# Attention with keys split ahead, score passes of 256 columns, and values one step later on TensorE

## What is computed

```python
q = layernorm(x); k = v = ctx_2048            # (16, 128, 256)
scores = einsum('bhqd,bhkd->bhqk', q, k) * 16 ** -0.5
scores = where(key > query, -inf, scores)
out = einsum('bhqk,bhkd->bhqd', softmax(scores), v)
x = x + tanh(g_xattn[1]) * out
```

## Time and profile before

| | us |
|---|---|
| median of 3 runs | 922.41 (921.37 to 923.53) |
| profiled execution | 921.7 |
| its span in the trace | 919.9 |

### The profile page before, as it was taken

One profiled execution on the slowest core, in us unless ns is written; L12 is line 12 of the kernel. 1 busy time (PEld: TensorE's weight loads), 2 busy tenths in 40 slices (PEclk: granted clock), 3 DMA queues, 4 the chain that ended last, 5 costly groups with the idle time before them and its releaser, 6 DMA issues.

```text
span 919.9 us, 13780 instructions
## 1 busy us (share of the span) xinstructions
PE 888.2 (97%) x4704; PEld 711.0 (77%) x4704; DVE 604.5 (66%) x1238; ACT 550.3 (60%) x955; POOL 191.7 (21%) x163
## 2 busy tenths in 40 slices
PE   6799999999999999989999989999999999999997
PEld 5699887787888888756666667878788888888886
DVE  6699764465645656598898776657765465665554
ACT  3225353434543344468888766777777877777774
POOL 5799200000000102067776420000000000000000
PEclk8899999999999999999999999999999999999999
DMA  8203150442211532135553334434444344444443
GB/s 299 76 14 121 41 149 18 132 121 81 74 53 50 182 104 64 40 115 172 173 165 126 113 96 140 124 121 141 133 150 143 102 134 144 145 138 147 150 127 103
DMA packets 62564, 108.54 MB, mean 118 GB/s; under 512 B 7808, under 2 KB 18432, under 8 KB 62112
## 3 DMA queue, kind: packets, MB, share of 16 engines
q1 hardware_dynamic: 61776, 107.53, 37.0%
q10 hardware_dynamic: 720, 0.14, 0.1%
HBM read 103.13 MB, written 4.52 MB: 117 GB/s over the span
## 4 chain that ended last, share of the span: by engine, by line
PE 84%; DVE 6%; ACT 3%; POOL 2%; DMA 2%; issue 2%; SPq 0%; DVEq 0%; ACTq 0%; POOLq 0%
PE bank L666 37%; PE bank L702 29%; PE bank L1470 2%; PE bank L1481 2%; PE bank L1153 1%; PE bank L1152 1%; PE bank L1150 1%; PE bank L1166 1%; PE bank L365 1%; PE bank L1463 1%; DMA k_blocks_sb<-in_k_blk 1%; PE bank L1462 1%; PE bank L1458 1%; DMA x_mixed<-in_x 1%; PE bank L346 1%
## 5 line engine op out<-in xcount | busy, mean ns | idle before, releaser
L465 ACT ACTIVATE y_hi<-y 128x512 fp32r<-128x512 f32 x200 | 124.1, 621 | 81.3 <-DVE y L546 80.7
L560 DVE TENSOR_TENSOR y<-y,gate_rows 128x512 f32<-128x512 f32 x124 | 85.8, 692 | 120.4 <-ACT y L454 118.2
L702 PE MATMUL bank<-y_hi,w_hi 128*128 128x512 f32 x400 | 157.3, 393 | 1.5 <-DVE y_lo L311 1.0
L702 PE MATMUL bank<-y_lo,w_hi 128*128 128x512 f32 x400 | 156.7, 392 | 0.0
L702 PE MATMUL bank<-y_hi,w_lo 128*128 128x512 f32 x400 | 156.1, 390 | 0.0
L311 DVE TENSOR_TENSOR y_lo<-y,y_hi 128x512 fp32r<-128x512 f32 x196 | 134.4, 686 | 29.9 <-ACT y_hi L465 29.6
L448 ACT ACTIVATE activated<-bank 128x512 f32<-128x512 f32 x136 | 81.1, 597 | 80.8 <-PE bank L666 76.2
L666 PE MATMUL bank<-x_hi_first,w_hi 128*128 128x512 f32 x264 | 106.3, 403 | 0.7 <-DVE w_lo L306 0.7
L666 PE MATMUL bank<-x_hi_first,w_lo 128*128 128x512 f32 x264 | 104.3, 395 | 0.0
L666 PE MATMUL bank<-x_lo_first,w_hi 128*128 128x512 f32 x264 | 104.2, 395 | 0.0
L666 PE MATMUL bank<-x_hi_last,w_hi 128*128 128x512 f32 x264 | 104.0, 394 | 0.0
(11 more groups left out here) (155 smaller groups left out, 1436.5 us busy)
## 6 DMA issues: line engine op xcount, KB each, us to landing
gate_rows<-gates SPq DMA_DIRECT2D x156, 256.0 KB, 3.7
w_raw<-in_wu SPq DMA_DIRECT2D x68, 256.0 KB, 2.6
k_blocks_sb<-in_k_blk SPq DMA_DIRECT2D x64, 256.0 KB, 4.6
w_raw<-in_wu SPq DMA_DIRECT2D x32, 384.0 KB, 3.2
v_slot<-in_v_rows SPq DMA_DIRECT2D x16, 256.0 KB, 2.6
ctx_windows<-in_ctx_win SPq DMA_DIRECT2D x3, 1024.0 KB, 10.8
toeplitz<-in_kpad SPq DMA_DIRECT2D x4, 512.0 KB, 9.1
x_mixed<-in_x SPq DMA_DIRECT2D x4, 512.0 KB, 9.2
```

Source lines behind the costliest of these rows:

```text
L465: act.activation(mem.yhi[:, K % S, :], mem.y[:, K % S, :], ACT.Copy).then_inc(s_yh, 1)
L560: dve.tensor_tensor(mem.y[:, K % S, :], mem.y[:, K % S, :], gate, ALU.mult).then_inc(s_yd, 1)
L702: last = pe.matmul(acc(s)[:, c, :], w_[:, Nu % S, wc], y_[:, K % S, :], start=(n == 0 and m == 0), stop=(n == U - 1 and m == 2), skip_grou ...
```

## The change

The keys are no longer split in the attention. The host passes them compactly (`k_rows`, 128 x 256 a block). In units 16 to 42 of `f0` they are loaded two blocks at a time into the slots of the values, rounded by ScalarE (`split_hi`), differenced by GpSimd (`split_lo`) and both parts are stored to DRAM (`k_parts`), four transfers each time. GpSimd sets the eight key slots to zero once. For a quad, `load_keys` now brings two 64-partition pieces of 64 KB, each part's rows repeated twice (by a step of zero in the source), into the non-zero halves; the slot is used by TensorE as it lands, and is free again after its scores.

The split of the work over the 128 rows changes with it: rows hold two heads, each with both parts of the keys against both parts of the query (which is laid out twice). So a score pass covers two heads, 256 columns, with its own stationary queries, and a quad has two of them in place of two of 512. The queries have two sets a = 0, 1, so there are two groups of four transposes and two copies per batch in place of one; they are now float32r transposes with a rounded identity. Rounding and difference of the queries are over 512 elements, before 256.

TensorE's order in step n becomes turns of n, scores of n+2, values of n-1. Of the query's groups, set 0 of b+2 stands at t = 3, set 1 of b+1 at t = 0. On ScalarE the query copies stand ahead of the exponential at t = 0 and 1, and the output copy behind it.

```diff
-                    if not final and K == NK - 16:
-                        attention_loads(sp)
+                    if not final:
+                        if K in (16, 18):
+                            load_raw(sp, (K - 16) // 2)
+                        if 21 <= K < 45 and K % 3 == 0:
+                            i = (K - 21) // 3
+                            store_parts(sp, i)
+                            if i + 2 < NB // 2:
+                                load_raw(sp, i + 2)
+                        if K == NK - 16:
+                            attention_loads(sp)
+                        if NK - 16 <= K < NK - 16 + KR:
+                            load_keys(sp, K - NK + 16)
...
+                    for i in range(NB // 2):
+                        split_lo(pool, i)
+                    blocks_zeroed(pool)
...
+                        if 19 <= K < 43 and K % 3 == 1:
+                            split_hi(act, (K - 19) // 3)
...
-        KLR, KR, SR, DR, PR = 6, 4, 3, 3, 3
+        KR, SR, DR, PR = 8, 3, 3, 3
...
-        KM = sb("k_blocks_sb", [P, KLR, 4 * P])
-        K1 = sb("k_blocks_hi", [P, KR, 4 * P], F32R)
-        K2 = sb("k_blocks_lo", [P, KR, 4 * P], F32R)
+        K1 = sb("k_blocks", [P, KR, 4 * P], F32R)
+        ident_r = sb("ident_r", [P, P], F32R)
+        xc = sb("xn_c", [P, 2, D])
         V = sb("v_slot", [P, 2, NH1, 32])
-        xc = sb("xn_c", [P, 2, D])
-        xs = sb("xn_split", [P, 2, 4, 2, 64], F32R)
-        Q1 = sb("q_split_t", [P, 2, 4, P], F32R)
+        xs = sb("xn_split", [P, 2, 4, 2, P], F32R)
+        Q1 = sb("q_split_t", [P, 2, 2, 4, P], F32R)
...
+        def split_places(i):
+            parts = xs[:, i % 2].rearrange("p t a f -> p (t a f)")
+            return V[:, i % 2].rearrange("p h d -> p (h d)"), parts[:, 0:2 * D], parts[:, 2 * D:4 * D]
+        def load_raw(sp, i):
+            if i >= 2:
+                sp.wait_ge(s_k2, i - 1)
+            sp.dma_start(split_places(i)[0].rearrange("p (b f) -> p b f", b=2),
+                         k_rows[2 * i:2 * i + 2].rearrange("b p f -> p b f")).then_inc(s_kr[i % 2], 16)
+        def split_hi(act, i):
+            act.wait_ge(s_kr[i % 2], 16 * (i // 2 + 1))
+            if i >= 2:
+                act.wait_ge(s_ks[i % 2], 64 * (i // 2))
+            raw, high, _ = split_places(i)
+            act.activation(high, raw, ACT.Copy).then_inc(s_k1, 1)
+        def split_lo(pool, i):
+            pool.wait_ge(s_k1, i + 1)
+            raw, high, low = split_places(i)
+            pool.tensor_tensor(low, raw, high.bitcast(F32), ALU.subtract).then_inc(s_k2, 1)
+        def store_parts(sp, i):
+            sp.wait_ge(s_k1, i + 1)
+            sp.wait_ge(s_k2, i + 1)
+            for part, rows in enumerate(split_places(i)[1:]):
+                for j in range(2):
+                    place = k_parts[2 * i + j].rearrange("(g s d) f -> g s d f", s=2, d=HD1)[:, part]
+                    sp.dma_start(place, rows[:, j * D:(j + 1) * D].bitcast(F32)).then_inc(s_ks[i % 2], 16)
+        def blocks_zeroed(pool):
+            pool.memset(K1[:].rearrange("p n f -> p (n f)").bitcast(F32), 0.0).then_inc(s_kz, 1)
         def load_keys(sp, n):
-            if n >= KLR:
-                sp.wait_ge(s_k2, n - KLR + 1)
-            sp.dma_start(KM[:, n % KLR, :], k_blk[n]).then_inc(s_kl[n % KLR], 16)
+            if n >= KR:
+                sp.wait_ge(s_s, n - KR + 1)
+            for hh in range(2):
+                first = k_parts.offset + (2 * P * (n // 4) + 64 * (n % 4) + 32 * hh) * D
+                place = bass.AP(k_parts.tensor, first, [[D, 2 * HD1], [0, 2], [1, D]])
+                sp.dma_start(K1[64 * hh:64 * hh + 64, n % KR, hh * D:hh * D + D].bitcast(F32), place).then_inc(s_kl[n % KR], 16)
 
         def load_values(sp, b):
             if b >= 2:
                 sp.wait_ge(s_pv, 4 * (b - 2) + 4)
             sp.dma_start(V[:, b % 2].rearrange("p h d -> p (h d)"), v_rows[b]).then_inc(s_vl[b % 2], 16)
-        def key_hi(act, n):
-            act.wait_ge(s_kl[n % KLR], LOADED + 16 * (n // KLR + 1))
-            if n >= KR:
-                act.wait_ge(s_s, n - KR + 1)
-            act.activation(K1[:, n % KR, :], KM[:, n % KLR, :], ACT.Copy).then_inc(s_k1, 1)
-        def key_lo(pool, n):
-            pool.wait_ge(s_k1, n + 1)
-            pool.tensor_tensor(K2[:, n % KR, :], KM[:, n % KLR, :], K1[:, n % KR, :].bitcast(F32),
-                               ALU.subtract).then_inc(s_k2, 1)
 
         def query_normed(act, b):
             act.wait_ge(s_sh, b // (2 * BPB) + 1)
@@ -1354,36 +1398,46 @@
             act.activation(xc[:, b % 2, :], X[:, b, :], ACT.Identity, bias=nshift[:, b:b + 1],
                            scale=rstd[:, b:b + 1]).then_inc(s_n, 1)
 
+        def copies_of(view):
+            return view.rearrange("p (g f) -> p g f", f=HD1).unsqueeze(2).broadcast_to((P, NH1, 2, HD1))
+        def part_rows(b, part):
+            return xs[:, b % 2].rearrange("p t a (h d f s) -> p (t a h) d f s", h=2, d=2, s=2)[:, :, :, :, part]
         def query_hi(act, b):
             act.wait_ge(s_n, b + 1)
             if b >= 2:
-                act.wait_ge(s_xt, b - 1)
-            act.activation(xs[:, b % 2, :, 0, :], xc[:, b % 2, :].rearrange("p (q f) -> p q f", q=4),
-                           ACT.Copy).then_inc(s_hi, 1)
+                act.wait_ge(s_xt, 2 * (b - 1))
+            else:
+                act.wait_ge(s_ks[b], 64 * (NB // 4))
+            act.activation(part_rows(b, 0), copies_of(xc[:, b % 2, :]), ACT.Copy).then_inc(s_hi, 1)
 
         def query_lo(pool, b):
             pool.wait_ge(s_hi, b + 1)
-            pool.tensor_tensor(xs[:, b % 2, :, 1, :], xc[:, b % 2, :].rearrange("p (q f) -> p q f", q=4),
-                               xs[:, b % 2, :, 0, :].bitcast(F32), ALU.subtract).then_inc(s_lo, 1)
-        def query_turned(pe, b):
+        def query_turned(pe, b, a):
...
-                last = pe.transpose(x_bank[:, t * P:(t + 1) * P],
-                                    xs[:, b % 2, t].rearrange("p s f -> p (s f)").bitcast(F32), ident[:])
+                last = pe.transpose(x_bank[:, t * P:(t + 1) * P].bitcast(F32R), xs[:, b % 2, t, a, :], ident_r[:])
...
+            act.wait_ge(s_xt, 2 * b + a + 1)
             if b >= 2:
                 act.wait_ge(s_s, 4 * (b - 1))
-            act.activation(Q1[:, b % 2].rearrange("p t q -> p (t q)"), x_bank, ACT.Copy, scale=SCALE1).then_inc(s_qt, 1)
+            act.activation(Q1[:, b % 2, a].rearrange("p t q -> p (t q)"), x_bank, ACT.Copy, scale=SCALE1).then_inc(s_qt, 1)
...
-            for n in range(KLR):
-                load_keys(sp, n)
+            for i in range(2):
+                sp.wait_ge(s_ks[i], 64 * (NB // 4))
+            sp.wait_ge(s_kz, 1)
...
-            if left in (12, 11, 4):
-                query_normed(act, {12: 0, 11: 1, 4: 2}[left])
-            if left in (11, 10, 3):
-                query_hi(act, {11: 0, 10: 1, 3: 2}[left])
-            if left in (9, 8, 7, 6):
-                key_hi(act, 9 - left)
-            if left in (6, 3):
-                query_copy(act, {6: 0, 3: 1}[left])
+            if left == 16:
+                act.activation(ident_r[:], ident[:], ACT.Copy).then_inc(s_ir, 1)
+            if left in (15, 13, 4):
+                query_normed(act, {15: 0, 13: 1, 4: 2}[left])
+            if left in (14, 12, 3):
+                query_hi(act, {14: 0, 12: 1, 3: 2}[left])
+            if left in (10, 7, 4, 1):
+                query_copy(act, (10 - left) // 6, (10 - left) // 3 % 2)
...
-            if left in (8, 5):
-                query_turned(pe, {8: 0, 5: 1}[left])
+            if left in (12, 9, 6, 3):
+                query_turned(pe, (12 - left) // 6, (12 - left) // 3 % 2)
...
-                pe.wait_ge(s_k2, n + 1)
+                pe.wait_ge(s_kl[n % KR], LOADED + 32 * (n // KR + 1))
                 if t == 0:
-                    pe.wait_ge(s_qt, b + 1)
-                pe.matmul(s_bank(n), Q1[:, b % 2, t, :], K1[:, n % KR, :], start=False, stop=False)
-                pe.matmul(s_bank(n), Q1[:, b % 2, t, :], K2[:, n % KR, :], start=False, stop=True).then_inc(s_s, 1)
+                    pe.wait_ge(s_qt, 2 * b + 2)
+                blocks = K1[:, n % KR, :].rearrange("p (h a k) -> p h a k", h=2, a=2)
+                for a in range(2):
+                    last = pe.matmul(s_bank(n)[:, a * 2 * P:(a + 1) * 2 * P], Q1[:, b % 2, a, t, :], blocks[:, :, a, :],
+                                     start=False, stop=(a == 1))
+                last.then_inc(s_s, 1)
...
-                    if n + KR < NQ:
-                        key_lo(pool, n + KR)
...
                     turned(pe, n)
                     if n + 2 < NQ:
                         scores(pe, n + 2)
-                    if n == 0:
+                    if n == 1:
                         pe.wait_ge(f0.s_xa, 5)
-                    if n < NQ - 1:
-                        values(pe, n)
+                    if n > 0:
+                        values(pe, n - 1)
...
```

(43 more changed lines are left out.)

17 lines of the change are left out of this document (10 added, 7 removed).

## The result

| | kernel before | changed kernel |
|---|---|---|
| median | 922.48 us (921.37 to 923.53) | 906.98 us (906.16 to 910.07) |
| ratio to before, 95% interval | | 0.9842 [0.9823, 0.9862] |
| profiled execution, its span | 921.7, 919.9 | 910.07, 908.3 |

The gain is 15.5 us where 11.4 were forecast; 907.0 lies inside the range and outside the forecast's own 908 to 914. So the two traces lie 11.6 us apart where the medians lie 15.5 apart.

What follows compares the result with a forecast made beforehand. The attention step was held bound by the 1.70 us latency chain turns, exponential, values, with TensorE close behind. Passes and order 17.4, query groups -6.2, key splitting 1.0, feed-forward -0.9 gave 11.3 us: forecast 911.0, range 904 to 920.

Steps and rivals of the forecast that it cites:

- The chain of 1.70: Attention step bound by turns, exponential, values, turns: 0.70 + 0.60 + 0.05 + 0.35 = 1.70 us; step becomes 1.40.
- The price of a query group: Attention: a group of four rounded query transposes taken at 0.44 us; 14 more groups cost 6.2 us.
- rounded transposes fast: Rival, chance 0.12: query transposes cost 0.06 us each, 5.7 us less over 27 groups, about 906.
- The sum: Whole kernel: 17.4 - 6.2 + 1.0 - 0.9 = 11.3 us gained; profiled 921.7 to 910.4, median 911.0.
- The score passes: Attention: two 256-column passes start 0.12 us apart, between bounds 0.115 (columns) and 0.19 (weight load).
- alone ... 4.6 us: Attention: moving values of n-1 into step n by itself cuts 0.41 to 0.33 us, 4.6 us over 58 steps.
- Keys late: Rival, chance 0.09: key halves landing after 3.19 us stall score passes; at 4.3, 15.5 us, 926; loses from 4.0.
- They bound nothing except once.: Attention: ScalarE's rounding and GpSimd's difference of keys, now removed, delayed only one score pass; counted 1.0 us gain.
- VectorE: Attention: 6.35 us a batch by starts, under TensorE's 6.92; rival with hand-overs, chance 0.12: 7.06 by durations, 913.
- The first feed-forward: 16 instead of 8 transposes lose 0.9 us; key splitting and stores there cost zero, bounds 0 to 4 us.
- The passage: From the first feed-forward's last output pass to the attention's first turns: no change forecast, 0 us.
- The clock: Rival, chance 0.01: fewer columns bring 1.2 GHz, doubling the array's 0.9 us of a step: 52 us, 963.

Runs made afterwards that it cites:

- The four passes: Changed kernel with four score passes of 128 columns in place of two of 256, same columns and scores: 916.2 us.
- the keys' way freed: Kernel before with the new order, value rows issued behind the keys of 4b+5, and key rounding ahead of the output copy: 916.1 us.
- the run with the keys first: Changed kernel with a batch's value rows issued behind the keys of 4b+6: 907.17 us.
- the passes alone: Changed kernel with the old order, values of n in step n and output copy ahead of the exponential: 931.45 us.
- the gap filled: Changed kernel with eight unused float32 products filling TensorE's idle time at the attention's start: 908.02 us.
- the run with both edits: Changed kernel with value rows issued behind later keys and TensorE's idle time ahead of the attention filled: 908.01 us.
- the chain only: Changed kernel with the old order, output copy ahead of the exponential, both query copies behind it: 925.9 us.
- the run with only the copy moved: Kernel before with the new order and key rounding moved ahead of the output copy, transfers as before: 931.17 us.

## Why the prediction was right, and where it was not

- *The chain of 1.70 and its end.* Right. The wait of the values is gone, the plain step is 1.39 against 1.40 from four spacings, and the run without the order has the 1.70 back. "Without the new order the chain of 1.70 would have held all of this back" is shown by 925.9 us.
- *The price of a query group.* The term that was mis-sized. A batch is 6.70 against 6.92: 0.18 of it are the two groups, by the run with float32 transposes, at 0.35 each and not 0.44. The stage gained 15.0 us and not 12.2. Of these 2.8 the price is 1.3 (104.74 against 103.41), or 2.0 without the stall for keys; the run that has the forecast's price is still 1.6 better than the forecast's stage of 106.3. Part of that is at the stage's end, where three long steps (60 to 62) shrank from 7.68 to 6.05, by 1.6 where the sum counts 3 x 0.30; the rest is spread over steps off the pattern. The rival "rounded transposes fast" had the sign and twice the size (0.21 less a group, measured 0.09); its time of 906 is nearer to the result than the forecast is.
- *The sum.* The forecast of 11.3 us between the profiled executions met 11.6. That is luck: the stage gave 2.8 more, and the pieces put at nothing or nearly (run variation at both ends, the low clock, the passage) took 2.5 of it. Between the medians, 2.8 of the 4.1 us beyond the forecast are the stage's; the rest lies in no piece that a trace shows.
- *The score passes.* Right: 0.115 (0.12 taken). The four passes put the least spacing of such passes at 0.11, just under it.
- *The order "alone ... 4.6 us".* The size was right (5.6 with the keys' way freed), the claim was not: made alone it costs 10 us. The step that failed is the sentence on the values: "Who waits for values now waits one step longer" named the output copy and its own readers, but not what is queued behind the two waiters. These are the keys behind the value rows on SP and the key rounding behind the output copy on ScalarE. The rival "Keys late" looked at SP's queue for the changed kernel only.
- *"They bound nothing except once."* It was read from the kernel before, and holds there. But the splitting of keys is what comes next: with the new order it holds 15.8 us back (931.9 against 916.1). So the splitting ahead, counted with 1.0 us, is what frees the order's gain in this change, and not a part beside it.
- *Keys late.* Nearly right. The landing is 2.4 us in the median, under the 3.19 of room, and 3.8 at the longest, above it; two passes in the stage waited for keys, 1.0 us in all, and the change would have lost only from a landing of 4.0 us on. The Trainium skill, "DMA: Bandwidth & Descriptors", Rules for kernel authors, advises against two transfers to disjoint partition halves. The trace shows them landing early enough here (2.4 us each, where the 256 KB keys before took 4.3), though SP spends twice the issues.
- *VectorE.* Right that it doesn't bind the batch; it was priced at 7.06 by durations as a rival, and the batch of 6.70 excludes that. But 6.70 against the 6.35 of its starts leaves 5%, and where it has other work (the norms of step 40) the step is now late by 0.4.
- *The first feed-forward.* 0.77 against 0.9 (1.09 in the run with float32 transposes), and no stall behind the stores.
- *The passage.* Missed: a query copy ahead of the table load cost 0.46 of 0.55 us. The text had counted this stage's moved copies by their sum on ScalarE, and not by who stands behind them.
- *The clock.* The rival of 52 us did not occur: 1.00 from turns 5 to 63. The Trainium skill, "TensorE: Matmul & The Clock Gate", Part 4, says that transposes do not count as activity; with four to eight of them and fewer score columns in each step, no fall came. What came was 6.8 us at 1.2 GHz behind an idle time, which no rival had.

## What to carry to other kernels

When a consumer is moved one step later, list every wait on its semaphore, and for each the instructions queued behind it on the waiting engine: here a transfer queue and a copy, each enough alone to cost more than the order gains. An edit whose engines "bound nothing" may still be what another edit of the same change needs; read it in the schedule after, not in the one before. Two causes of a loss can hide each other, so removing one and seeing nothing doesn't clear it.

## What the runs showed of the hardware

- *Rounded transposes.* Four float32r transposes of 128 x 128 cost 0.09 us less a group than four float32 ones (batch 6.70 against 6.88 with two groups). Their weight loads start 0.085 us apart, the float32 ones 0.11.
- *The clock after a short idle.* Behind the idle time at the attention's start a fall to 1.2 GHz came in three profiles: the changed kernel, idle 1.91 us; the run with the keys first, 1.95; and, for 3.4 us, the passes alone, 1.96. It stayed away with the gap filled, in the run with both edits, and with 1.36 and 1.44 us of idle; but it stayed away too in the runs with float32 transposes, 1.95, with the chain only, 1.91, and with four passes, 1.79. So an idle time of 1.9 us goes with the fall but does not decide it; what does is open. A fourth fall, of 6.8 us, stands inside the stage of the run with only the copy moved, at 468.26 us, near the end of 2.48 us in which TensorE waited for a key.
- *VectorE beside GpSimd.* The update of X, between SBUF operands, takes 0.48 us alone and up to 1.62 beside an operation of GpSimd. In the fourteen traces 45 updates took over 0.6 us, and each ends 0.28 us after a GpSimd operation that began before it or within 0.05 us of its start: the update waits for GpSimd rather than running slowly beside it. Where the update began earlier than that, it kept its 0.48, and GpSimd's operation took up to 1.60 in place of 1.28. The maxima and subtractions, which read PSUM, keep 0.63 to 0.69 beside the same work.
- *SP.* The 64 KB key transfers took SP 0.6 us each in a burst, longer than the 256 KB ones before (0.47).
